# Ten first-pass products of attention unit 0 moved in between the down products of the first feed-forward block

## The reference

```python
x = L0_attn_qkv                      # 4 x 1024 x 128
x = x + 0.5 * _L0_ffn_ref(_layernorm(x, axis=-1), ...)
x = x + _L0_attn_ref(_layernorm(x, axis=-1), ...)
x = x + 0.5 * _L0_ffn_ref(_layernorm(x, axis=-1), ...)
```

```python
scores = jnp.einsum('bhgqd,bhkd->bhgqk', qg, k) * scale
bias = jnp.where(causal, slopes.reshape(KVH, G, 1, 1) * rel, -jnp.inf)
attn = jax.nn.softmax(scores + bias[None], axis=-1)
out = jnp.einsum('bhgqk,bhkd->bhgqd', attn, v)
```

## Time and profile before

| what | value |
|---|---|
| median of 3 runs | 719.02 us (716.4 to 719.27) |
| the profiled execution | 714.09 us |
| its span, first to last instruction | 712.3 us |
| mean granted TensorE clock | 0.988 |
| down phase and its tail | from 92.3 us to 173.0 us of the span |
| one attention unit, in the middle of the program | 25.7 us |

### The profile page before, as it was taken

One profiled execution on the slowest core, in us unless ns is written; L12 is line 12 of the kernel. 1 busy time (PEld: TensorE's weight loads), 2 busy tenths in 40 slices (PEclk: granted clock), 3 DMA queues, 4 the chain that ended last, 5 costly groups with the idle time before them and its releaser, 6 DMA issues.

```text
span 712.3 us, 15912 instructions
## 1 busy us (share of the span) xinstructions
PE 688.1 (97%) x5892; PEld 359.0 (50%) x5892; DVE 569.5 (80%) x1886; ACT 403.1 (57%) x581; POOL 139.1 (20%) x157
## 2 busy tenths in 40 slices
PE   8999999978999999999999999999999999999998
PEld 4554488843344444444444444444444456544597
DVE  6977337698999999999999999999999667675311
ACT  3353344224776776777777777677677664353200
POOL 3201895562000000000000000000000012104950
PEclk9999999996999999999999999999999999999999
DMA  8012542544001001101100100100110000005731
GB/s 225 0 18 62 103 77 87 161 138 136 21 21 40 21 21 41 28 22 31 41 20 21 40 21 22 39 22 20 41 30 12 1 2 0 2 5 102 105 89 60
DMA packets 47249, 34.69 MB, mean 49 GB/s; under 512 B 13106, under 2 KB 46514, under 8 KB 47172
## 3 DMA queue, kind: packets, MB, share of 16 engines
q1 hardware_dynamic: 46596, 33.60, 19.2%
q10 hardware_dynamic: 576, 0.08, 0.1%
HBM read 23.01 MB, written 10.39 MB: 47 GB/s over the span
## 4 chain that ended last, share of the span: by engine, by line
PE 60%; DVE 15%; issue 13%; DMA 4%; SPq 3%; POOL 2%; ACT 2%; DVEq 0%; ACTq 0%; POOLq 0%
PE ps L1103 56%; DVE mx L969 8%; PE ps L1108 4%; POOL h_all L504 2%; DMA mask_second<-sel_scr 2%; DVE mx L962 1%; DMA yT<-sel_scr 1%; DMA k_scr<-kp 1%; SPq L401 1%; DVE xn L748 1%; DVE h_all L962 1%; ACT h_all L666 1%; SPq L398 1%; DVE stats L736 1%; DVE wb L989 0%
## 5 line engine op out<-in xcount | busy, mean ns | idle before, releaser
L666 ACT ACTIVATE h_all<-ps 128x1024 f32<-128x1024 f32 (+3 forms) x384 | 291.6, 810 | 112.9 <-PE ps L1103 109.3
L969 DVE TENSOR_REDUCE mx<-ps 128x1 f32<-128x512 f32 (+2 forms) x352 | 223.0, 681 | 9.6 <-PE ps L1103 6.7
L1103 PE MATMUL ps<-ks,xnT_all 57*128 57x512 bf16 (+3 forms) x768 | 176.3, 333 | 10.1 <-DVE mx L962 5.1
L1103 PE MATMUL ps<-h_all,vb 128*32 128x512 f32 (+3 forms) x1536 | 163.2, 498 | 1.0 <-ACT osb L655 1.0
L1103 PE MATMUL ps<-xnT_all,ks 59*128 59x512 bf16 (+3 forms) x768 | 157.9, 331 | 0.7 <-ACT h_all L666 0.4
L962 DVE CUSTOM_DVE_ANT_0 h_all<-ps,mask_w 128x384 bf16<-128x384 f32 (+1 forms) x256 | 149.1, 618 | 2.7 <-issue 1.0
L1103 PEld LDWEIGHTS ps<-ks,xnT_all 57*128 57x128 bf16 x768 | 56.1, 94 | 135.7 <-DVE mx L962 62.5
L1103 PE MATMUL ps<-cb 64*128 64x64 bf16 (+3 forms) x1216 | 112.1, 214 | 0.0
L594 ACT ACTIVATE sg<-ps 128x512 f32<-128x512 f32 x80 | 47.8, 597 | 82.6 <-PE ps L1103 82.3
L766 DVE TENSOR_TENSOR h_all<-ps,sg 128x512 f32<-128x512 f32 x80 | 55.1, 690 | 47.8 <-PE ps L1103 46.1
L1103 PEld LDWEIGHTS ps<-cb 64*128 64x128 bf16 x1216 | 79.7, 96 | 16.8 <-issue 0.4
(11 more groups left out here) (129 smaller groups left out, 537.2 us busy)
## 6 DMA issues: line engine op xcount, KB each, us to landing
xnT_all<-q_scr SPq DMA_DIRECT2D x64, 96.0 KB
attn<-sel_scr SPq DMA_DIRECT2D x12, 256.0 KB, 7.0
mask_second<-sel_scr SPq DMA_DIRECT2D x12, 256.0 KB, 7.8
q_scr<-qp SPq DMA_DIRECT2D x8, 384.0 KB
ks<-k_scr SPq DMA_DIRECT2D x64, 48.0 KB
x<-in_x SPq DMA_DIRECT2D x8, 256.0 KB, 6.2
yT<-sel_scr SPq DMA_DIRECT2D x8, 256.0 KB, 8.9
q_scr<-qp SPq DMA_DIRECT2D x8, 256.0 KB
```

What stands on the lines that cost most here:

```text
L666: act.activation(pr[:, (NSTEP * i + s) % PR_BUFS, p:HPG:SLOTS, lo:HALF], ps[:, b:b + 2, lo:HALF], ACT.Exp)\
L969: dve.tensor_reduce(m, src, AX.X, V.max).then_inc(a_out, 1)
L1103: return pe.matmul(o, l, r, start=start, stop=stop, skip_group_check=True)
```

## The change

`EARLY` gets a third place, after the first quarter of a down product, and larger numbers. Before the change two places per group were used: before the last quarter, and behind `project`. The diff is whole:

```diff
-EARLY = [(0, 0), (0, 0), (0, 0), (0, 0), (2, 2), (2, 3), (2, 3), (2, 3)]
+EARLY = [(0, 0, 0), (0, 0, 0), (0, 0, 0), (0, 0, 0), (2, 3, 3), (2, 3, 3), (2, 3, 3), (0, 2, 3)]
...
-TAIL = (3, 3)
+TAIL = (2, 1)
...
-assert FIRST_HALF <= early(GROUPS - 1, 1).start and LAST_SPLIT < NP1
+assert FIRST_HALF <= early(GROUPS - 1, 2).start and LAST_SPLIT < NP1
...
                             ln_apply(c, par, f.rs2, f.Tb, f.xn2)
+                        early_maxima(early(c, 1))
                         if not first:
                             (middle if c > 1 else split)(c - 1, 1 - par)
                             values(c - 1, (c - 1) // 2, 1 - par)
-                        early_maxima(early(c, 1))
+                        early_maxima(early(c, 2))
...
                             xn_T(c - 2)
+                        if transpose and t == 1:
+                            early_pieces(early(c - 1, 0))
                         if transpose and t == GT - 1:
-                            early_pieces(early(c - 1, 0))
+                            early_pieces(early(c - 1, 1))
...
                     if qkv and last:
                         xn_T(c - 1)
-                        early_pieces(early(c, 0))
+                        early_pieces(early(c, 1))
                     if qkv and not first:
                         project(c - 1, 1 - par)
-                        early_pieces(early(c, 1))
+                        early_pieces(early(c, 2))
```

## The result

| | before | after |
|---|---|---|
| median, 20 executions each, same chip | 716.63 us (715.0 to 720.29) | 720.0 us (717.69 to 722.44) |
| ratio, 95% interval | | 1.0044 [1.0033, 1.0055] |
| the profiled execution (span) | 714.09 us (712.3) | 718.07 us (716.3) |
| its mean granted clock | 0.988 | 0.983 |

The change makes the kernel slower by 0.44%, 3.2 us of 716.6: forecast were 2.3. The ratio and its interval are worked out from all executions of both kernels, so it is not the quotient of the two medians (these stand 3.4 us apart). The two profiled executions stand 4.0 us apart, and both are among the fastest of their kernels: 2.5 us under the median before, 1.9 us after.

The account below looks back on a forecast made before the run. PE was taken to bound the down products, with DVE behind it and SP's queue as a hidden third limit. Score step 4's +2.3 us delay, carried to the end and put on the 719.02 us median, gave 721.3 us, range 717.5 to 725.0.

Parts of the forecast that it names:

- the gate: On SP, the second maxima's load behind the landing of group 7's store makes score step 4 2.3 us later; chance 0.5.
- The upper end of the range: 725.0 us: the clock at 5 us of low stretch, with a fourth of a per cent for the runs.
- Groups 4 and 5: Added DVE reductions partly fill waits for queries; `x` of group 5 comes 1.0 us later, of group 6 0.7.
- Group 6, the ring: Group 5's query product 3.5 us later: 2.0 from ten products, 1.5 from PE waiting for reductions to free banks.
- Group 7: Norm unchanged at 2.48 us, two new 384 reductions behind it cost 0.97 us; `xn_T(7)` 3.4 us later.
- The store of group 7: Projection, split and store follow `xn_T(7)` by the same 3.4 us, putting the store at 173.3 us.
- SP's queue: First maxima's load at 170.8 us, first score 0.8 us later; second load behind the stores, step 4 at 183.1 us.
- The stores *are* the gate: Answers the rival that SP's work ends in time and the saved reductions count: about 718 us, chance 0.2.
- The plain saving: Rival: ten reductions hidden in DVE's waits, none given back; 4.2 us less, 714.8 us, chance 0.06.
- The rule weighed against a row: Judging PE by weight loads, 14% free, the ten products cost nothing; sum 1 to 2 us lower, about +1.
- The clock rival: Low PE clock moves past step 4, costing 1.5 to 2.5 us more: 723.3 us, chance 0.22.
- After step 4: Work order unchanged and PE nearly full, so step 4's 2.3 us delay carries to the end.

Follow-up runs that it names:

- e5: Kernel before, with SP issuing the second maxima's load ahead of its wait for all stores: 717.21 us, ratio 1.0007 to before.
- e4: Changed kernel keeping the third place, but with the old product numbers per group, without the ten more ahead: 717.52 us, ratio 1.001 to before.
- e8: Changed kernel plus unread filler products in PE's gaps up to group 7's transposes: median 716.44 us, ratio 1.0029 to before.
- e1: Changed kernel, with SP issuing the second maxima's load ahead of its wait for all stores: 717.0 us, ratio 1.0008 to before.
- e6: Changed kernel with the second maxima's load ahead of the store wait and middle(7) ahead of values(7): 716.07 us, ratio 0.9991 to before.
- e3: Changed kernel with middle(7) on DVE ahead of group 7's values and three reductions: 718.14 us, ratio 1.0023 to before.
- e7: Kernel before with the second maxima's load ahead of the store wait and middle(7) ahead of values(7): 715.84 us, ratio 0.9999 to before.
- e2: Changed kernel plus four unread filler products of 512 columns on PE between products 26 and 27: 721.19 us, ratio 1.006 to before.
- e12: Changed kernel with load and split moved ahead, PE gaps filled, also ahead of products 24 and 25: 716.01 us, ratio 0.9991 to before.

## Why the prediction was right

The time (720.0 us, forecast 721.3, range 717.5 to 725.0) and the sign came out, and the gate is the one named as the likeliest. That the time came so near was in part luck: the forecast put +2.3 us on a median of three runs, 719.02 us; the median of twenty is 716.63, and on that the same sum gives 718.9 us, 1.1 under the result: a loss taken too small and a start taken too high cancelled in part. The upper end of the range, by its own terms, is 719.02 + 2.3 + 2.5 + 1.8 = 725.6 us and not 725.0, on which nothing hangs. Step by step, profile of after against the text:

- **Groups 4 and 5.** `x` of groups 5 and 6 was forecast 1.0 and 0.7 us late, it was 1.3 and 1.2: in group 5's body the wait for the queries took up less. Right within half a us.
- **Group 6, the ring.** Query product of group 5 at 149.73 us, forecast 149.0; `x` of group 7 at 154.49, forecast 153.9, 3.3 us late and not 2.7. The 0.6 us are for the most part carried over from the group before, by reductions 16 and 17. The query product was 4.2 us late and not 3.5, and the split of that was off: from group 2's query product to group 5's PE took 24.20 us before and 28.45 after. In that stretch PE's weight loads waited for reductions four times (0.43, 0.28, 0.23 and 0.47 us), never before the change. So the ring's waits were real, but at most 1.4 us over three bodies, 0.7 of it in group 6's, where 1.5 was taken; and the ten products took at least 2.8 us of PE, not 2.0. The price of 0.20 us was read from five products of one matmul each; 16 and 17, which pack blocks and add their masks by a second matmul, took 1.04 us together (143.72 to 144.76), at most 0.23 of it waiting.
- **Group 7.** From `x` to the norm 3.41 us (3.40 taken), the norm 2.47 (2.48 taken). `xn_T(7)` at 164.54, forecast 163.8 (3.4 late, measured 4.2). Of the 0.8 us, 0.6 come from `x`.
- **The store of group 7: mis-sized.** "The projection, the split ... 3.4 us later", so 173.3 us; it was 175.32, 5.4 us late. The step that was off is that everything behind `xn_T(7)` follows it at the distance read from the profile of before. From `xn_T(7)` to the store were 9.53 us before and 10.78 after, 1.25 us more: the values and keys products at the half clock take 1.00 us more, and `middle(7)` stands behind the keys. But this is a property of that one execution more than of the change: in e5, the old order at the half clock, the distance is 10.63 us (162.26 to 172.89), in e4 10.64. The order itself adds some 0.15 us. I had looked for the clock only behind step 4, where PE has no cover, and not ahead, where it makes SP's queue late, in either order. e8 shows the price: 1.84 us of the store's time.
- **SP's queue.** The first maxima's load at 171.49 (170.8), the first score 1.1 us late (0.8). The landings: a store 2.64 us (2.36 taken), a maxima load 1.81 us where I took 2.3 between bounds of 0.7 and 2.36. Step 4 at 184.99 us instead of 183.1, 4.2 us late in the profiled execution; by the ratio the loss is 3.2. The gate itself is shown: e1 and e6 take it away and with it the loss, e3 makes it come earlier, e5 and e7 find nothing to take away before.
- **The rivals.** The stores *are* the gate: that falls by e1 against e5. The plain saving isn't there even without it: e6 against e7 leaves 0.6 us of the 4.2, 1.9 at the most. The rule weighed against a row, that free weight loads let PE take the ten products for nothing, would have put the loss near 1 us; the interval of 2.4 to 3.9 us (0.33 to 0.55%) excludes it as the result, and the stretch above, with at least 2.8 us of PE for the ten, contradicts its ground. The clock rival, with low clock after step 4, is not in the profile of after (1.00 from 185 to 190 us) but happened in e2, at 2.5 us, within the 1.5 to 2.5 given.
- **After step 4.** "I carry the delay to the end": step 4 is 4.2 us late, the first output transposes 4.0 (213.72, before 209.70), the span 4.0. Right.

Not settled: how the 3.2 us divide between the delay of `xn_T(7)` and the clock's, since both act through the one store, and the profiled pair sets an execution of before with a high clock against one of after. The profile of after is 1.9 us under its median; whether in the slower executions the low clock reached past step 4, as the clock rival has it, no trace shows. And it is open whether, without the wait for the stores, the new order is better at all.

## What to carry to other kernels

Before moving work ahead of a late producer, follow every queue that stands behind it: here 4.3 us saved on DVE turned into a loss of 3.2, because the DMA that released the next stage stood on SP behind the landing of the delayed stores. Without that wait the saving and the delay about cancelled. A small DMA that releases compute should be issued ahead of a wait for bulk stores, where its own data allow it. When one gate is taken away, look for the next at once (here the first maxima's load), and time the same edits on the old kernel too, or a repaired loss is taken for a gain.

## What the runs showed of the hardware

- **The clock differs between executions of one kernel.** In e8 the same program ran at a mean of 0.993 to 0.995 or 0.983 to 0.986 and took some 716.3 or 722.5 us; of 35 of before, those at 0.975 or 0.976 took 717.4 to 719.2 us and the two at 0.988 some 713.9. The profile of before, at 0.988, is such a favourable draw, and e5, its equal up to group 5's query product, ran at 0.979 and took 3.0 us longer. A difference of 3 us is told by many executions, not by two profiles.
- **Filling one gap is no guarantee.** 3.7 us of matmuls kept the clock at 1.00 across the gap, and it fell 3 us later, behind shorter ones. Only e12, which fills the most gaps, had a mean clock of 0.993 or more in all executions, and even there it was at 0.59 from 175 to 180 us.
- **The norm's length depends on its neighbours.** The four instructions of 128x128 take 2.47 us in group 7's body, where POOL works on the split from 157.87 us to 160.3, but 1.11 us in groups 5 and 6, where POOL's last work ends just before (at 137.95 and 148.04 us). That POOL is the cause is likely, not tested. Timeline of DVE after:

```profile
138.08 1.11 DVE L748 TENSOR_SCALAR xn<-x,mv,rstd 128x128 f32<-128x128 f32 x4
...
148.14 1.11 DVE L748 TENSOR_SCALAR xn<-x,mv,rstd 128x128 f32<-128x128 f32 x4
```
